# Vision tower on one core: front attention and search tiles in other slots, keys masked by head on another engine

## The reference, cut to what is computed

```python
h = h + attn(layernorm(h))    # 8 heads of 8: normalised q and k, position bias, softmax, projection
h = h + ffn(layernorm(h))

# ffn, for each of 8 heads and each token:
q = (x @ Wq) * 64 ** -0.5
scores, idx = top_k(sim with 2 x 64 product keys, 16)       # each side
final, where = top_k(all sums of the two sides, 16)         # of 4096 keys a head
w = softmax(final)
k = sum(w * keys_table[where]); v = sum(w * values_table[where])
out = causal_softmax(q @ k.T) @ v
```

## Time and profile before

| | |
|---|---|
| median of 3 runs | 3051.8 us (3051.78 to 3052.03) |
| the profiled execution's own time | 3053.45 us |
| its span, first to last instruction | 3051.4 us |
| granted TensorE clock, mean | 0.998 |
| instructions | 60054 |

### The profile page before, as it was taken

How to read it: one execution, slowest core, us unless ns; L and a number is a source line. 1 busy time by engine, 2 the same in 40 slices (tenths; PEclk the granted TensorE clock), 3 DMA queues, 4 the chain that set the end, 5 groups by cost and what they waited for, 6 DMA issues and landing times.

```text
span 3051.4 us, 60054 instructions
## 1 busy us (share of the span) xinstructions
PE 2907.5 (95%) x16560; PEld 1968.0 (64%) x16560; DVE 2554.1 (84%) x10286; ACT 1730.3 (57%) x4926; POOL 1569.5 (51%) x3406
## 2 busy tenths in 40 slices
PE   8999999999999999999999999999999999999998
PEld 7867656665666566656665666566656666776666
DVE  4677789988998899889988898889888987777776
ACT  4465565555555555556555655565556555655554
POOL 2234356655665566555655565556655654333331
PEclk9999999999999999999999999999999999999999
DMA  9213211121111211121112111211121111010100
GB/s 214 50 45 79 52 31 33 32 37 34 32 32 31 41 29 32 32 40 30 30 31 45 25 32 32 40 31 33 32 38 33 33 33 38 20 24 20 25 20 19
DMA packets 121289, 117.47 MB, mean 38 GB/s; under 512 B 61491, under 2 KB 109310, under 8 KB 120958
## 3 DMA queue, kind: packets, MB, share of 16 engines
q1 hardware_dynamic: 105525, 83.84, 12.9%
q0 software_dynamic: 14336, 29.39, 5.6%
q10 hardware_dynamic: 1096, 0.41, 0.1%
HBM read 66.36 MB, written 9.84 MB: 25 GB/s over the span
## 4 chain that ended last, share of the span: by engine, by line
PE 53%; DVE 23%; issue 9%; POOL 7%; ACT 7%; ACTq 0%; DMA 0%; DVEq 0%; POOLq 0%
PE ps L831 27%; PE ps L819 11%; DVE wts L1230 11%; ACT wts L1005 4%; DVE x_sum L1297 2%; PE ps L755 2%; DVE top L1214 2%; PE ps L724 2%; PE ps L772 1%; PE ps L706 1%; POOL stat L528 1%; PE ps L862 1%; DVE cand_rest L1216 1%; DVE rest L1196 1%; POOL stat L525 1%
## 5 line engine op out<-in xcount | busy, mean ns | idle before, releaser
L831 PE MATMUL ps<-wts,table 128*128 128x455 f32 (+2 forms) x5120 | 2006.0, 474 | 0.0
L1230 DVE SCALAR_TENSOR_TENSOR wts<-ps,wts 128x455 f32<-128x455 f32 (+2 forms) x2560 | 1349.9, 531 | 383.4 <-ACT wts L1005 372.6
L819 PE MATMUL ps<-st,spread 128*128 128x456 f32 (+2 forms) x2560 | 1237.4, 483 | 119.0 <-DVE wts L1230 110.1
L1005 ACT ACTIVATE wts<-ps 128x455 f32<-128x455 f32 (+2 forms) x2560 | 1126.6, 475 | 86.8 <-PE ps L819 78.5
L831 PEld LDWEIGHTS ps<-wts,table 128*128 128x128 f32 x5120 | 905.4, 190 | 104.1 <-issue 44.4
L819 PEld LDWEIGHTS ps<-st,spread 128*128 128x128 f32 x2560 | 482.2, 188 | 603.0 <-DVE wts L1230 524.3
L591 POOL DMA_INDIRECT x_rows<-folded,x_r x448 | 453.8, 1013 | 85.9 <-issue 80.9
L524 POOL TENSOR_SCALAR stat<-top 110x1 f32<-110x1 f32 (+1 forms) x268 | 70.7, 264 | 760.1 <-DVE top L1214 756.2
L511 POOL TENSOR_TENSOR cand<-best 110x15 f32<-110x15 f32 (+5 forms) x804 | 160.4, 226 | 221.0 <-DVE best L1198 219.5
L980 ACT ACTIVATE cand_e<-top,stat 110x16 f32<-110x16 f32 (+1 forms) x268 | 82.3, 307 | 297.1 <-POOL stat L531 296.3
L976 ACT ACTIVATE sc<-ps 110x128 f32<-110x128 f32 (+1 forms) x268 | 74.2, 277 | 255.9 <-PE ps L772 255.6
(11 more groups left out here) (186 smaller groups left out, 3762.3 us busy)
## 6 DMA issues: line engine op xcount, KB each, us to landing
st<-st SPq DMA_DIRECT2D x320, 114.0 KB, 2.3
table<-in_table SPq DMA_DIRECT2D x128, 128.0 KB, 5.0
rz_row<-rz_dram SPq DMA_DIRECT2D x52, 165.0 KB
folded<-table SPq DMA_DIRECT2D x64, 128.0 KB, 2.6
x_rows<-folded,x_r POOLq DMA_INDIRECT x448
rz_row<-rz_dram SPq DMA_DIRECT2D x28, 228.0 KB
scratch<-in_x SPq DMA_DIRECT2D x7, 343.0 KB, 4.5
rz_dram<-rz SPq DMA_DIRECT2D x52, 1.3 KB
```

Source lines behind the costliest of these rows:

```text
L819: mm(ps[0:128, g % NA, 0:t], spread[:, q * 128:(q + 1) * 128], st[:, k % 2, ORDER[c // QUADS], 0:t], start=True, stop=True).then_inc(a_rea ...
L831: mm(ps[0:128, ACC + k % 2, 0:t], table[:, k % H, i, :], wts[:, g % RING, 0:t], start=(c == 0), stop=(c == CH - 1)).then_inc(out_done, 1)
L1005: A(wts[:, g % RING, 0:t], ps[0:128, g % NA, 0:t], ACT.Exp).then_inc(e_ready, 1)
L1230: V.scalar_tensor_tensor(out=wts[:, g % RING, 0:t], in0=ps[0:128, g % NA, 0:t], scalar=0.0, in1=wts[:, g % RING, 0:t], op0=ALU.is_ge, op1= ...
```

## The change

Three things. `ATT` goes from `LN1 + 28` to `LN1 + 35`, so that all attention tasks, the projection and the second layernorm stand seven slots later (the tasks' scores in slots 3 and 19 of a head, no more 12 and 28, and the layernorm ends in slot 208, no more 201). The search tiles and `pick` start 15 slots ahead, no more 16: one slot later with all their steps. And the keys of one head are masked on ScalarE, as a copy with the head's 0-or-1 column as its scale, no more as a product on GpSimd; distance -2, waits and semaphore are the same. On ScalarE it is issued after the norms' square root and ahead of the tasks' exp.

```diff
@@ -93,13 +93,14 @@
 BIAS_PITCH = H * (2 * L - 1)
 SCR = 4
 
-TILE_START = {CH * (k - 1) - 16 + 8 * (t + sparse(k)): (k, t) for k in range(HEADS) for t in range(tiles(k))}
-PICK_START = {CH * (k - 1) - 16: j for j, k in enumerate(PICKS)}
+LEAD = 15
+TILE_START = {CH * (k - 1) - LEAD + 8 * (t + sparse(k)): (k, t) for k in range(HEADS) for t in range(tiles(k))}
+PICK_START = {CH * (k - 1) - LEAD: j for j, k in enumerate(PICKS)}
 OUT, BEST, CAND, TOP, SHIFT, ZSUM, HIGH, ZINV, LOW, TURN, TURNED = 1, (2, 3, 5), 6, 8, 13, 14, 15, 16, 16, 18, 19
 
 ROWS = 22
 MAPS, TOK, LN1 = ROWS + 3, ROWS + 6, ROWS + 10
-QK, VAL, NRM, ATT = LN1 + 11, LN1 + 14, LN1 + 17, LN1 + 28
+QK, VAL, NRM, ATT = LN1 + 11, LN1 + 14, LN1 + 17, LN1 + 35
 PERIOD = 16
 
 X_OUT, X_BEST, X_CAND, X_INDEX, X_WHERE, X_TOP = 1, 2, 7, 8, 9, 9
@@ -486,14 +487,6 @@
                     P.tensor_copy(inv[:, 0:n, :].rearrange("p b (h d) -> p b h d", d=HD),
                                   by_image(nrm[:, 0:n * 2 * H], n).unsqueeze(3).to_broadcast([L, n, 2 * H, HD]))\
                         .then_inc(nrm_spread, 1)
-                j = task_at(p, q, -2)
-                if j is not None:
-
-                    pool.wait_ge(qk_unit, 2 * p + 2)
-                    if j >= 1:
-                        pool.wait_ge(s_mm, base + j)
-                    P.tensor_scalar(kx[0:C, 0:t], xf[:, 0:t], head_of[0:C, j:j + 1], None, ALU.mult)\
-                        .then_inc(kx_ready, 1)
                 j = task_at(p, q, 3)
                 if j is not None:
                     pool.wait_ge(s_red, base + j + 1)
@@ -945,6 +938,13 @@
                 if q == NRM + 1:
                     act.wait_ge(nrm_mm, p + 1)
                     A(nrm[:, 0:n * 2 * H], ps[0:L, FR, 0:n * 2 * H], ACT.Sqrt).then_inc(nrm_ready, 1)
+                j = task_at(p, q, -2)
+                if j is not None:
+
+                    act.wait_ge(qk_unit, 2 * p + 2)
+                    if j >= 1:
+                        act.wait_ge(s_mm, base + j)
+                    A(kx[0:C, 0:t], xf[:, 0:t], ACT.Copy, scale=head_of[0:C, j:j + 1]).then_inc(kx_ready, 1)
                 j = task_at(p, q, 5)
                 if j is not None:
                     act.wait_ge(s_sub, base + j + 1)
```

## The result

The changed kernel takes 3142.9 us (median of 4 runs, 3140.44 to 3146.95) against 3051.91: ratio 1.0299, 95% interval 1.0287 to 1.0311. It is 91 us slower; I had forecast 24 us faster, and the range ended at 3068. Its profiled execution took 3141.26 us, with a span of 3139.4.

What follows compares the result with a forecast made beforehand. VectorE was taken to bound task heads, waits for ScalarE's exp the others. Terms sum to -3.9 us per seven-image pass, -27.3 for seven; +1.5 other passes, +1.4 prologue: -24.4, so 3027.4 us; own range 3008 to 3045, overall 2998 to 3068.

Steps and rivals of the forecast that it cites:

- (a): GpSimd-VectorE locks on x_sum and x_acc products: of 10.0 us surplus a seven-image pass, 3.0 stay; counted -6.0.
- (c): Task add and maximum no longer cover VectorE's search-tile waits: +2.0 us a seven-image pass, bounds 0 and 5.0.
- (d): Masked-key copy on ScalarE, ahead of the exp of slots 2 and 18: +0.9 us a pass, bounds 0 and +4.3.
- The sign that I had tied to (c): Sign of a wrong forecast: VectorE's idle time in heads 2 and 3 risen to 6 us, the cover gone.
- (b): ScalarE's copy L1017 moves ahead of the tile's exp sum L980, into its wait: -2.1 us a pass, bounds -4.2 and 0.
- (e): Task score matmuls pile up in TensorE's slot 3, VectorE's first add waits: +0.8 us a pass, bounds -1.0 and +1.6.
- The prologue's first unit: Start of the first unit after the prologue: later by +0.7 for pass 0's tail and +0.7 for a fold copy.
- The slower side: Rival "ScalarE late", 24%: each copy before an exp delays a mask by its whole 0.54 us; 3073 us.
- The price per event that I set: In the ScalarE-late rival: about 0.45 us of delay per copy decides against the change.

Runs made afterwards that it cites:

- the repair: Changed kernel with the task's exp L951 one slot later on ScalarE and its row sum and reciprocal one slot later on VectorE: 3067.41 us, ratio 1.0041.

## Why the prediction was wrong

(a), the locks, was right in kind and size: I left 3.0 of 10.0 us of surplus and forecast VectorE at near 270 us a pass; it is 270.58. Head 2's x_sum is 5.24 (forecast 5.6), head 3's x_acc 3.70 (4.8). That the remainder fits is partly luck: at the places where I left 0.75 us each there is no surplus, and the 2.7 us that are left stand in x_acc of heads 2 and 4, behind the gather and the subtraction of slot 22.

**The step that failed is in (a) too, and in what (c) and (d) did not take from it.** I worked out that L550 and L501 run back to back behind the threshold and end 3.7 us after the last maximum, and asked of that only whether it blocks VectorE's products. I did not ask who waits for L501: ScalarE's exp L951, two slots on, ahead of a unit's exp. In its place the runs showed this: ScalarE's idle time before L951 went from 1.0 to 45.1 us, VectorE's idle time before masks 9 and 25 of the task heads from 5.4 to 78.4 over the run, and with that exp one slot later 64 of the 91 us are back. The section on the kernel before even says that a step that is not ready holds everything behind it. I applied this to the step whose place I looked at because it was moved to another engine (the copy) and to the search tile's (L1017 behind L980), not to the steps of a task, which moved as a block. The forecast net of everything but locks was +2.1 us a pass; measured, VectorE's idle time rose by 14.8. The sign that I had tied to (c), idle time of 6 us in heads 2 and 3, came close: it rose to 4.5 and 6.8 us. With the task's exp one slot later VectorE's idle time before the masks of these heads falls from 4.0 and 5.3 us to 1.8 and 3.0, so most of the rise was this queue and not lost cover.

(b), L1017 ahead of L980: idle before masks 15 and 16 over a pass went from 6.3 to 4.4 us, so 1.9 against the 2.1 taken. (c) was of the right sign and far too small, because I counted cover lost, not waits gained. (d), the copy: ScalarE's lasts longer than the 0.54 us that I took,

```profile
L947 ACT ACTIVATE kx<-hx,head_of 64x455 f32<-64x455 f32 (+1 forms) x80 | 50.7, 634 | 0.1
```

but it costs nothing and gains 7 us in the old slots. By the Trainium skill, page "SBUF — State Buffer", section on SBUF's two separate sides, a VectorE instruction with two SBUF inputs and a GpSimd one that reads SBUF exclude each other for the whole instruction. The traces agree in part, as the rows before did: the product did not block for its length (the copy alone takes 5 us off VectorE's 2554), while the subtractions did, before (1.60 us) and after (the x_acc product of 1.70 us in head 2). (e): VectorE's idle time before the tasks' first add (L1141) is 0.3 us a pass and before masks 4 to 6 of the task heads nothing, so the pile of score matmuls starves nobody, and thinning it did harm; the output matmuls, whose move I took for a possible gain, now keep L1165 waiting 2.3 us a pass, and before they did not. The prologue's first unit starts at 137.94 instead of 134.58 us, 3.4 later where I had 1.4.

**The rivals.** The slower side had the right engine, ScalarE's queue, and the wrong step: I priced the copy, whose inputs were 14 slots old, and gave it 24%. The price per event that I set, an exp held by half a microsecond, is less than what L951 does: of the 1.70 us before mask 9 in head 3 it is 0.91, its wait of 0.33 and its own 0.58, just what the repair took away. The range ended at 3068, even below that rival's 3073, and no case of mine had a wait with a late input on it.

**Why both moves together.** Part of this is shown and part is open. Shown is what the exp's place costs: L951 stands ahead of a unit's exp in a slot where ScalarE is already late, because GpSimd's threshold, or its subtraction behind the threshold, is late; moved behind that exp it gives back most of the loss, and little in the old slots. The shift puts L501 in a slot with the FFN subtraction, and the later tiles put the threshold's five instructions ahead of both, as the timeline shows. But this meeting in one slot is not needed: the run with six slots has no such meeting and loses 58 us, the one with tasks two slots earlier has no FFN attention in it and loses 49. The two moves cost 96 us together and 17 apart. Of the difference 31 us are lock savings that do not add, and the rest is idle time of VectorE; no run splits that rest by engine. What remains after the repair (ratio 1.0041) is as large as the shift alone costs; its cause is open.

## What to carry to other kernels

In an order written out by hand, moving a block of steps moves each step's place in every engine's queue: for each, ask when its input is ready at the new place, what already waits ahead of it, and what of the critical loop stands behind it. Put a step that waits for a slow engine behind, not ahead of, the loop's own instruction of the next slot; here that, with the sums that read it, is worth 0.4% in good slots and 2.6% in bad ones. Two moves that are each nearly free can be dear together, perhaps since slack in a queue is spent once; that reason is a reading, not a measurement.

## What the runs showed that I had not expected

The gains of removing lock stalls don't add (33, 22 and 42 us less VectorE work for both moves, shift alone and tiles alone, all with the product on GpSimd), and a stall's length depends on what GpSimd has in front and on when VectorE arrives: in the same slot 1.60 us behind a gather, 0.54 without. ScalarE's copy with a column as its scale took 0.634 us on average, longer than the tasks' exp of the same width from and to SBUF without one (0.540 in the kernel before), and under half of GpSimd's 1.353. The changed kernel's four runs spread over 6.5 us, the kernel before's over 0.25.
